# Setup per block of eight row tiles, sums copied bank by bank, last messages written into SBUF: two graph layers on one core

## The chip, the cores and the metric

One Trainium2 chip, one of its cores. The metric is the device time of the whole program in microseconds (us). Its engines are TensorE (PE, with PEld for its weight loads), VectorE (DVE), ScalarE (ACT), GpSimd (POOL) and SyncE (SP), which here only issues loads.

## What is computed

Two layers over 8192 nodes with 128 features, and one 8192 x 8192 adjacency matrix of zeros and ones in float32 (256 MB):

```
h  = relu(layernorm(x));  Wh = h @ W
e  = leaky_relu(Wh@a1 + (Wh@a2).T, 0.2)
att = softmax(where(adj > 0, e, -9e15))
x  = x + relu(att @ Wh)
h  = relu(layernorm(x));  node = h @ W1            # 16 heads
y  = sum over k of node[:, k] * (h @ W2[k])        # the "messages"
x  = x + relu(adj @ y + node @ b)
```

## The kernel before, in words

Rows are cut into 8 blocks (NB) of 8 tiles (T) of 128 rows; NT = 64 tiles. The order on each engine is written out by hand, with semaphores; no scheduler moves anything. A wait on an engine holds all that stands behind it there. There are four stages.

**Setup.** SyncE loads x into `wh` (eight loads), then W, a1, a2, b, W1 and W2, then adj. VectorE takes the statistics of all 64 tiles (L806), aggregates them all (L811), ScalarE takes one square root (L445), then the loop `project` runs over the blocks: VectorE normalises eight tiles into `xn8` (L820), TensorE transposes them (L648), ScalarE applies relu (L451) into `hT4`, TensorE multiplies each tile by `w_sb`, 128 columns (L655), and by `wa` = W [a1 a2], 2 columns (L656), ScalarE copies Wh back over x (L455). Then ScalarE casts the first adj parts to bytes (`cast`, L467, seven times), VectorE finds the extremes of f1 and f2 (L831 to L851), ScalarE takes three exponentials (L485 to L488): `bcol` for the Wh rows, `qcol` and `zcol` for the weights. VectorE multiplies all eight blocks of Wh by `bcol` (L857). `zcol` is transposed, stored to HBM (L495) and read back by GpSimd, spread over all partitions (`load_z`, L401).

**Attention**, 8 target blocks x 4 turns (`IT`) x 2 parts p x 4 chunks k (C). Per chunk TensorE transposes one piece of the byte mask (`turn_mask`, L683), ScalarE evicts it (`evict`, L479), VectorE makes the weights of two source tiles, `p_sb` = max(z, q) times mask (`weigh`, L896), and TensorE adds 2 x 8 products of 129 columns (Wh and the row sum) into three banks `ot_ps` (L734). ScalarE casts adj ahead; it also stores the turned mask to HBM (`maskT_d`, L548) for the second layer. From the second block on the tiles of the block before are finished beside it (`finish_tile`, k = 0 to 3): VectorE divides, adds x (`xt`) and normalises; TensorE multiplies by W1 and W2 (L694, L699); ScalarE scales 16 heads (L525); GpSimd folds them (L381, L384), cuts the message into a high and a low part (L388, L390) and stores it (`msg_d`, L393) with the rows to keep (`keep_d`, L398). `confirm` counts the stores that have landed in `kept`. At a block's end ScalarE copies the three banks to `ut` (L571, in `end_block`), and TensorE clears the banks for the next block (L716, in `start_block`, after the wait on `ot_copied`). ScalarE then loads `xt` for the tiles to finish (L531).

**First gather** (`gather(0, True)`): TensorE multiplies the messages of 64 tiles by masks turned back to float32 (`convert`, L584 and L945) for two of the eight blocks (L774), while the last block's eight tiles are finished, one per seven tiles. `msgs` lies over `wh` and the masks, so SyncE loads messages (L306) once all reads of these are past, eight tiles at a time, each behind its `kept` count. **Three more gathers** of two blocks follow, and the results are turned and added.

## Time and profile before

| | us |
|---|---|
| median of 3 runs (lowest, highest) | 1968.48 (1953.25, 1979.71) |
| profiled execution | 1956.41 |
| its span | 1954.8 |

The mean granted clock of TensorE over the span was 0.983 of full speed. The page gives the busy time of each engine as a share of the span; `PE` records in the timeline carry an `x` count of instruction records, and a float32 matmul leaves two records. A line ends with the idle time before it and what ended that. For stages the order of time is: setup to 121 us, attention from 121.6 to 1405, first gather from 1416 to about 1590, the other gathers to the end.

### The profile page before, as it was taken

The numbers are of one execution on the slowest core, as the hardware profiler recorded it, in microseconds if no ns is written. First come the engines' busy times: TensorE is split into PE (matmuls) and PEld (weight loads), VectorE is DVE, ScalarE is ACT, GpSimd is POOL, SyncE is SP. The second block draws the span as 40 slices with busy tenths as digits, with TensorE's granted clock in tenths as the row PEclk, the third lists the DMA queues.
The fourth block names the chain that finished last, engine by engine and source line by source line (L and its number), as shares of the span: only waits on it lengthen the run. The fifth ranks groups of instructions, "written<-read, shape, count | busy, mean of one in ns | idle before, by whom it ended". The sixth has DMA issues, their size and how long they took to land.

```text
span 1954.8 us, 38986 instructions
## 1 busy us (share of the span) xinstructions
PE 1831.2 (94%) x13412; PEld 1602.2 (82%) x13412; DVE 1206.2 (62%) x1511; ACT 1325.7 (68%) x2127; POOL 698.8 (36%) x533
## 2 busy tenths in 40 slices
PE   1869999999999999999999999999799889999998
PEld 1859988988889888898898898898677568888886
DVE  5356667767767776676676677676656434443434
ACT  1466678778777887787888787778455445555554
POOL 0000025645554554565465465464535400000000
PEclk9979999999999999999999999999999989999999
DMA  8078876776777767767767677673841084444340
GB/s 281 1 275 324 321 307 253 293 283 246 295 268 266 292 248 279 292 248 283 286 259 291 260 278 286 237 288 147 323 166 60 19 330 185 155 168 172 142 180 22
DMA packets 106481, 454.82 MB, mean 233 GB/s; under 512 B 6896, under 2 KB 15296, under 8 KB 88512
## 3 DMA queue, kind: packets, MB, share of 16 engines
q1 hardware_dynamic: 87472, 357.66, 49.4%
q10 hardware_dynamic: 11600, 75.54, 9.3%
q0 software_dynamic: 7360, 20.98, 2.8%
q8 instruction: 30, 0.49, 0.1%
q14 instruction: 19, 0.16, 0.0%
HBM read 366.04 MB, written 88.11 MB: 232 GB/s over the span
## 4 chain that ended last, share of the span: by engine, by line
PE 90%; issue 2%; DMA 2%; ACT 2%; DVE 1%; SPq 1%; POOL 1%; ACTq 0%; DVEq 0%; POOLq 0%
PE ot_ps L734 46%; PE mt_ps L774 12%; PE ot_ps L774 12%; PE hw_ps L699 11%; PE mt_ps L683 6%; PE ot_ps L655 1%; PE h_ps L694 1%; DMA xt<-in_x_dram 1%; ACT prod L525 1%; SPq L278 1%; ACT wh_mask L467 1%; PE mt_ps L648 1%; POOL prod L381 0%; DMA adj_sb<-maskT_d 0%; PE hw_ps L656 0%
## 5 line engine op out<-in xcount | busy, mean ns | idle before, releaser
L734 PE MATMUL ot_ps<-wh_mask,p_sb 128*128 (+1 forms) x8192 | 983.1, 278 | 3.6 <-DVE p_sb L896 3.6
L734 PEld LDWEIGHTS ot_ps<-wh_mask,p_sb 128*128 128x128 f32 x8192 | 945.0, 193 | 5.3 <-issue 3.5
L896 DVE SCALAR_TENSOR_TENSOR p_sb<-zb,qcol,mt 128x1024 f32<-128x1024 uint8 (+1 forms) x512 | 776.0, 1546 | 271.2 <-ACT mt L479 214.2
L381 POOL TENSOR_TENSOR prod<-prod 128x1024 f32<-128x1024 f32 (+2 forms) x192 | 409.2, 2131 | 537.7 <-ACT prod L525 527.3
L467 ACT ACTIVATE wh_mask<-adj_sb 128x2048 uint8<-128x2048 f32 x256 | 491.6, 1926 | 0.0
L584 ACT ACTIVATE mask<-adj_sb 128x1024 fp32r<-128x1024 uint8 x240 | 255.2, 1064 | 196.3 <-PE ot_ps L774 177.6
L479 ACT ACTIVATE mt<-mt_ps 128x1024 uint16<-128x1024 uint16 x256 | 266.8, 1043 | 169.7 <-PE mt_ps L683 160.4
L945 DVE CAST mask<-adj_sb 128x1024 fp32r<-128x1024 uint8 x272 | 200.9, 746 | 270.9 <-PE mt_ps L774 246.4
L525 ACT ACTIVATE prod<-hw_ps,node 128x128 f32<-128x128 f32 x1024 | 277.9, 382 | 100.5 <-PE hw_ps L699 100.5
L774 PE MATMUL mt_ps<-mask,msgs 128*128 128x512 f32 x1024 | 284.3, 400 | 30.0 <-DVE mask L945 29.0
L774 PE MATMUL ot_ps<-mask,msgs 128*128 128x512 f32 x1024 | 276.2, 392 | 0.7
L774 PEld LDWEIGHTS mt_ps<-mask,msgs 128*128 128x128 f32 x1024 | 191.9, 189 | 80.3 <-issue 41.9
L699 PE MATMUL hw_ps<-wcat,hT 128*128 128x512 f32 x512 | 240.7, 593 | 0.0
L774 PEld LDWEIGHTS ot_ps<-mask,msgs 128*128 128x128 f32 x1024 | 192.9, 189 | 43.8 <-issue 3.4
L683 PEld LDWEIGHTS mt_ps<-ident,wh_mask 128*128 128x128 bf16 x2048 | 144.7, 114 | 59.8 <-issue 58.2
L683 PE MATMUL mt_ps<-ident,wh_mask 128*128 128x128 bf16 x2048 | 157.3, 221 | 0.0
L699 PEld LDWEIGHTS hw_ps<-wcat,hT 128*128 128x128 f32 x512 | 88.8, 191 | 61.7 <-issue 61.1
L401 POOL DMA_DIRECT2D zb<-zrow_d x8 | 4.3, 541 | 243.1 <-DVE p_sb L896 131.2
L384 POOL TENSOR_TENSOR msg<-prod 128x128 f32<-128x128 f32 x64 | 80.4, 1256 | 5.0
L390 POOL TENSOR_TENSOR msg<-msg 128x128 fp32r<-128x128 f32 x64 | 71.5, 1117 | 5.1
L388 POOL CAST msg<-msg 128x128 fp32r<-128x128 f32 x64 | 58.3, 911 | 10.7 <-POOL msg L384 10.7
L393 POOL DMA_DIRECT2D msg_d<-msg x64 | 37.8, 590 | 47.2 <-ACT keep L517 25.9
(106 smaller groups left out, 631.5 us busy)
## 6 DMA issues: line engine op xcount, KB each, us to landing
adj_sb<-in_adj_dram SPq DMA_DIRECT2D x128, 2048.0 KB, 8.4
maskT_d<-mt ACTq DMA_DIRECT2D x64, 1024.0 KB, 5.3
adj_sb<-maskT_d SPq DMA_DIRECT2D x32, 2048.0 KB, 8.0
msg_d<-msg POOLq DMA_DIRECT2D x64, 128.0 KB, 6.0
keep_d<-keep POOLq DMA_DIRECT2D x64, 128.0 KB, 6.1
msgs<-msg_d SPq DMA_DIRECT2D x8, 1024.0 KB, 10.0
p_sb<-keep_d SPq DMA_DIRECT2D x4, 2048.0 KB, 12.5
wh_mask<-in_x_dram SPq DMA_DIRECT2D x8, 512.0 KB, 7.2
```

What stands on the lines that cost most here:

```text
L381: pool.tensor_tensor(prod[:, 0:n, :], prod[:, 0:n, :], prod[:, n:2 * n, :], ALU.add)\
L384: pool.tensor_tensor(msg32[:, :], prod[:, 0, :], prod[:, 1, :], ALU.add).then_inc(prod_read, 1)
L467: ins = act.activation(m8[:, q // 2, t:t + HT // 2, :].rearrange("p t n -> p (t n)"), adj_sb[:, q, part * (HT // 2) * BLK:(part + 1) * (HT ...
L479: act.activation(mt[:, p, k, :], mt_ps[k % 2][:, :].bitcast(U16), ACT.Copy).then_inc(evicted, 1)
L525: ins = act.activation(prod[:, head, :], hw_ps[g % 2][:, j * D:(j + 1) * D], ACT.Copy, scale=node[:, head:head + 1])
L584: act.activation(mask32[:, r, ib, :], masks[:, s % 4, ib, t % T // 2, :, t % 2], ACT.Copy)\
L683: ins = pe.transpose(words[:, t * P:(t + 1) * P], m8[:, p, t, :].bitcast(BF16)[:, k:BLK // 2:C], ident16[:, :])
L699: pe.matmul(hw_ps[g % 2][:, :], hT[:, :], wcat[:, g * HB:(g + 1) * HB], start=True, stop=True)\
L734: ins = pe.matmul(ot_ps[h][:, (t - t0) * ROW:(t - t0 + 1) * ROW], p_sb[:, r, t * P:(t + 1) * P], rows, start=False, stop=end and t == t1 - 1)
L774: ins = pe.matmul(acc_ps[2 * ib + h][:, :], msgs[:, t, c, :], mask32[:, r, ib, h * HB:(h + 1) * HB], start=t == 0 and c == 0, stop=t == NT ...
L896: dve.scalar_tensor_tensor(p_sb[:, r, :], zbf[:, bass.ds((ib % 2) * BLK, BLK)], qcol[:, bass.ds(tile + b_, 1)], mtb[:, p, k, :, b_], ALU.m ...
L945: dve.tensor_copy(mask32[:, r, ib, :], masks[:, s % 4, ib, t % T // 2, :, t % 2])\
```

## The change

1. **Setup per block.** Statistics, aggregation and square root are taken block by block, in the order statistics(i+1), norm(i); each x load has its own semaphore. `xn8` has two buffers. `wx_sb` holds W and W [a1 a2] side by side: one matmul of 130 columns per tile instead of two. A row of `whx` is 130 words instead of 129 and holds Wh, f1, f2; `fcol` is a view of it. TensorE turns the next block between the matmuls of this one. ScalarE casts a part of adj after each block from the second on. The parameter loads are issued by ScalarE.
2. **Scaling and z.** VectorE scales Wh blocks 0 and 1, GpSimd blocks 2 to 7; TensorE waits for these from the second turn on. The first block's z rows are spread by eight matmuls into `hw_ps` and two copies, without the trip to HBM.
3. **Block ends.** ScalarE copies each bank when it is done (`copy_sums`, in the last chunk, ahead of the last products), TensorE clears each bank when it is copied. `xt` is loaded one chunk earlier.
4. **Last messages.** For the last eight tiles GpSimd writes the parts straight into `msgs`; TensorE waits for each tile's cut. SyncE loads seven message slots, then the masks, with nothing between.
5. Two mask conversions ahead of the wait for the last sums, on VectorE and ScalarE.

```diff
-        wh_mask = sb("wh_mask", [P, NT * (D + 1) + BLK * T // 2])
+        wh_mask = sb("wh_mask", [P, NT * (D + 2) + BLK * T // 2])
+        wx_sb = sb("wx_sb", [P, D + 2])
...
-        whx = wh_mask[:, 0:NT * (D + 1)].rearrange("p (n f) -> p n f", f=D + 1)
+        whx = wh_mask[:, 0:NT * (D + 2)].rearrange("p (n f) -> p n f", f=D + 2)
+        fcol = whx[:, :, D:D + 2]
...
-            for s in range(NB):
+            for s in range(NB - 1):
                 sp.wait_ge(kept, (s + 1) * T + 2)
                 load_messages(s)
-                if s >= 4:
-                    load_masks(0, s)
+            for s in range(4, NB):
+                load_masks(0, s)
...
+            pool.wait_ge(wh_copied, 3 * NB)
+            pool.wait_ge(setup_act, 7)
+            for i in range(2, NB):
+                rows = wh[:, T * i:T * (i + 1), :]
+                pool.tensor_tensor(rows, rows, bcol[:, T * i:T * (i + 1)].unsqueeze(2).to_broadcast([P, T, D]),
+                                   ALU.mult).then_inc(wh_scaled2, 1)
             pool.wait_ge(z_stored, 16)
-            load_z(0)
...
-            finish_block(NB - 1)
-            confirm(1, IT * NB + 1)
+            for mi in range(T):
+                u, p, m = (NB - 1) * IT + mi // 2, mi % 2, (NB - 1) * T + mi
...
+                fold(m)
+                pool.wait_ge(prod_read, m + 2)
+                pool.tensor_copy(msgs[:, m, 0, :], msg32[:, :]).then_inc(cut_step, 1)
+                pool.wait_ge(cut_step, 2 * m + 1)
+                pool.tensor_tensor(msgs[:, m, 1, :], msg32[:, :], msgs[:, m, 0, :].bitcast(FP32), ALU.subtract)\
+                    .then_inc(cut_step, 1)
...
+            ahead = [(q, part) for q in range(4) for part in range(2 if q < 3 else 1)]
+            deviation(0)
+            for i in range(NB):
+                if i + 1 < NB:
+                    deviation(i + 1)
+                project(i)
+                if i:
+                    cast(*ahead[i - 1], 1, 0)
+            evict(0, 0, 0, 0)
+            evict(1, 1, 0, 0)
...
+            for h in range(2):
+                act.wait_ge(z0_done, h + 1)
+                act.activation(zbf[:, h * HB:(h + 1) * HB], hw_ps[h][:, :], ACT.Copy).then_inc(z0_copied, 1)
...
+            def copy_sums(ib):
+                if not (isinstance(ib, int) and ib == 0):
+                    act.wait_ge(u_read, T * ib)
+                    act.wait_ge(den_read, ib)
+                for h, (t0, t1) in enumerate(GROUPS):
+                    if h < 2:
+                        act.wait_ge(ot_done, 2 * ib + h + 1)
+                    else:
+                        act.wait_ge(p_used[3], 4 * IT * (ib + 1))
+                    act.activation(ut[:, t0:t1, :].rearrange("p t f -> p (t f)"),
+                                   ot_ps[h][:, 0:(t1 - t0) * ROW], ACT.Copy).then_inc(ot_copied, 1)
...
+            def turn_x(i, g):
+                pe.wait_ge(xn8_done, i + 1)
+                if i:
+                    pe.wait_ge(hT_done, 2 * (i - 1) + g + 1)
+                for j in range(4):
+                    ins = pe.transpose(mt_ps[g][:, j * D:(j + 1) * D], xn8[:, i % 2, 4 * g + j, :], ident[:, :])
+                ins.then_inc(xnT_done, 1)
+
             def project(i):
+                for g, (t0, t1) in enumerate(GROUPS):
+                    if i:
+                        pe.wait_ge(wh_copied, 3 * (i - 1) + g + 1)
+                    for t in range(t0, t1):
+                        pe.wait_ge(hT_done, 2 * i + t // 4 + 1)
+                        ins = pe.matmul(ot_ps[g][:, (t - t0) * (D + 2):(t - t0 + 1) * (D + 2)],
+                                        hT4[:, t // 4, t % 4 * P:(t % 4 + 1) * P], wx_sb[:, :], start=True, stop=True)
+                        if t == t1 - 1:
+                            ins.then_inc(wh_done, 1)
+                        if t % 4 == 3 and i + 1 < NB:
+                            turn_x(i + 1, t // 4)
...
             def start_block(ib, last):
-                if not (isinstance(ib, int) and ib == 0):
-                    pe.wait_ge(ot_copied, 3 * ib)
                 for h in range(3):
+                    if not (isinstance(ib, int) and ib == 0):
+                        pe.wait_ge(ot_copied, 3 * ib - 2 + h)
...
+                if not finish and not (isinstance(jg, int) and jg == 0):
+                    pe.wait_ge(wh_scaled2, NB - 2)
...
-                    if t % T == 0:
+                    if s == NB - 1:
+                        pe.wait_ge(cut_step, 2 * t + 2)
+                    elif t % T == 0:
                         pe.wait_ge(msgs_in[s], 16)
```

How the written order moves, at three places. ScalarE in the setup before: after the projection loop come the seven casts (`wh_mask<-adj_sb`), then the exponentials (L485 to L488).

```order
L459 REGISTER_ALU
L459 COMPARE_AND_BRANCH
L467 ACTIVATE wh_mask<-adj_sb 128x2048 x7
L485 ACT_TABLE_LOAD
L485 ACTIVATE bcol<-fcol,shifts 128x64
L486 ACTIVATE qcol<-fcol,shifts 128x64
L488 ACTIVATE zcol<-zcol 128x64
```

ScalarE in the setup now, the last two blocks of the projection and what follows.

```order
L485 ACTIVATE p_sb<-p_sb,eps 128x8
L493 ACTIVATE p_sb,hsum<-mt_ps 128x512 x2
L497 ACTIVATE wh_mask<-ot_ps 128x390 x2
L497 ACTIVATE wh_mask<-ot_ps 128x260
L505 ACTIVATE wh_mask<-adj_sb 128x2048
L493 ACTIVATE p_sb,hsum<-mt_ps 128x512 x2
L497 ACTIVATE wh_mask<-ot_ps 128x390 x2
L497 ACTIVATE wh_mask<-ot_ps 128x260
L505 ACTIVATE wh_mask<-adj_sb 128x2048
L517 ACTIVATE mt<-mt_ps 128x1024 x2
L530 ACT_TABLE_LOAD
L530 ACTIVATE zcol<-zcol 128x64
```

One cast stands behind each block, and the two evictions (L517) are ahead of the exponentials. At the end of a middle block ScalarE had, before, the last products (`prod`), then the copies of the sums (`ut`).

```order
L479 ACTIVATE mt<-mt_ps 128x1024
L522 REGISTER_ALU
L525 ACTIVATE prod<-hw_ps,node 128x128 x4
L522 REGISTER_ALU
L525 ACTIVATE prod<-hw_ps,node 128x128 x4
L566 ISA
L568 REGISTER_ALU
L571 ACTIVATE ut<-ot_ps 128x387 x2
L571 ACTIVATE ut<-ot_ps 128x258
```

Now:

```order
L517 ACTIVATE mt<-mt_ps 128x1024
L585 ISA
L588 ACTIVATE ut<-ot_ps 128x387
L585 REGISTER_ALU
L588 ACTIVATE ut<-ot_ps 128x387
L587 ISA
L588 ACTIVATE ut<-ot_ps 128x258
L568 REGISTER_ALU
L571 ACTIVATE prod<-hw_ps,node 128x128 x4
L568 REGISTER_ALU
L571 ACTIVATE prod<-hw_ps,node 128x128 x4
```

The three copies stand ahead of the last eight products. SyncE at the first gather had, before, masks (`adj_sb<-maskT_d`) between the messages:

```order
L306 DMA msgs<-msg_d 128x2048 x5
L321 DMA adj_sb<-maskT_d 128x2x4096
L306 DMA msgs<-msg_d 128x2048
L321 DMA adj_sb<-maskT_d 128x2x4096
L306 DMA msgs<-msg_d 128x2048
L321 DMA adj_sb<-maskT_d 128x2x4096
L306 DMA msgs<-msg_d 128x2048
L321 DMA adj_sb<-maskT_d 128x2x4096
L327 DMA p_sb<-keep_d 128x4096
```

Now:

```order
L306 DMA msgs<-msg_d 128x2048 x7
L322 DMA adj_sb<-maskT_d 128x2x4096 x4
L328 DMA p_sb<-keep_d 128x4096
```

The last message load is gone, and the four mask loads stand behind the seventh.

## Rows read from the trace of the kernel before

**Rows 1.** The page, busy us of each engine (share of the span) xinstructions.

```profile
PE 1831.2 (94%) x13412; PEld 1602.2 (82%) x13412; DVE 1206.2 (62%) x1511; ACT 1325.7 (68%) x2127; POOL 698.8 (36%) x533
```

**Rows 2.** Timeline of the setup: start us, us, engine, line, out<-in, count.

```profile
18.69 2.03 DVE L806 BATCH_NORM_STATS2 p_sb<-wh_mask  x8 [18.69 <-DMA wh_mask<-in_x_dram]
...
36.37 4.32 DVE L811 BATCH_NORM_AGGREGATE p_sb<-p_sb 128x2 f32<-128x6 f32 x64
...
41.69 2.14 DVE L820 TENSOR_SCALAR p_sb<-wh_mask,p_sb 128x128 f32<-128x128 f32 x8
```

**Rows 3.** Timeline of the projection, at the low and then the full clock.

```profile
53.87 0.60 ACT L451 ACTIVATE p_sb<-mt_ps 128x512 f32<-128x512 f32 x1 [0.45 <-PE mt_ps L648]
...
54.61 0.80 PE L655 MATMUL ot_ps<-w_sb,p_sb 128*128 128x128 f32 x2
...
55.48 0.77 PE L655 MATMUL ot_ps<-w_sb,p_sb 128*128 128x128 f32 x2
...
64.25 0.47 PE L655 MATMUL ot_ps<-w_sb,p_sb 128*128 128x128 f32 x2
...
64.69 0.47 PE L655 MATMUL ot_ps<-w_sb,p_sb 128*128 128x128 f32 x2
```

**Rows 4.** Timeline of the setup's end; the last row is of the chain.

```profile
93.66 12.69 ACT L467 ACTIVATE wh_mask<-adj_sb 128x2048 uint8<-128x2048 f32 x7
...
106.36 1.28 ACT L485 ACT_TABLE_LOAD   x1
...
108.40 9.17 DVE L857 TENSOR_TENSOR wh_mask<-wh_mask,bcol  x8 [11.84 <-ACT zcol L488]
...
121.64 5.75 PE L734 MATMUL ot_ps<-wh_mask,p_sb 128*128 128x129 f32 x32 [1.50 <-DVE p_sb L896]
...
127.84 3.63 PE ot_ps L734 x32
```

**Rows 5.** Timeline of VectorE and GpSimd near 379; last, the page's group of all products.

```profile
377.82 1.25 DVE L896 SCALAR_TENSOR_TENSOR p_sb<-zb,qcol,mt 128x1024 f32<-128x1024 uint8 x1
379.51 2.87 DVE L896 SCALAR_TENSOR_TENSOR p_sb<-zb,qcol,mt 128x1024 f32<-128x1024 uint8 x1 [0.44 <-PE ot_ps L734]
...
378.63 2.66 POOL L381 TENSOR_TENSOR prod<-prod 128x1024 f32<-128x1024 f32 x1 [7.67 <-ACT prod L525]
...
L896 DVE SCALAR_TENSOR_TENSOR p_sb<-zb,qcol,mt 128x1024 f32<-128x1024 uint8 (+1 forms) x512 | 776.0, 1546 | 271.2 <-ACT mt L479 214.2
```

**Rows 6.** Waits of TensorE, 120 to 1400 us: total us, times, longest.

```profile
PE ot_ps L716 <- ACT ut L571: 15.9, 7, 2.4
PE ot_ps L734 <- DVE p_sb L896: 3.6, 6, 1.5
```

**Rows 7.** Timeline at the end of the second block.

```profile
418.49 1.20 ACT L571 ACTIVATE ut<-ot_ps 128x387 f32<-128x387 f32 x3
...
419.75 0.82 PE L716 MATMUL ot_ps<-zeros 128*128 128x512 bf16 x3 [2.45 <-ACT ut L571]
```

**Rows 8.** The chain of waits at the start of the first gather.

```profile
1406.22 8.12 DMA xt<-in_x_dram
...
1416.20 2.04 PE mt_ps L774 x4
...
1421.64 0.93 PE mt_ps L774 x4
```

**Rows 9.** Timeline of TensorE at the last messages.

```profile
1573.15 2.05 PE L774 MATMUL mt_ps<-mask,msgs 128*128 128x512 f32 x4 [18.03 <-DVE mask L945]
```

**Rows 10.** Loads of x and of the messages, by line: ns, first and last start; landing.

```profile
L278 SPq DMA_DIRECT2D wh_mask<-in_x_dram x8: 658/1700/1992, 1.0 to 11.2; - x8
...
DMA to landing us min/median/max: 4.3/7.2/7.8
...
L306 SPq DMA_DIRECT2D msgs<-msg_d x8: 328/448/650, 1404.4 to 1562.4; - x8
...
DMA to landing us min/median/max: 4.9/10.0/14.7
```

More of the change, by code:

```diff
@@ L107, in build @@
         rstd = sb("rstd", [P, 1])
-        fcol = sb("fcol", [P, NT, 2])
         bcol = sb("bcol", [P, NT])
@@ L674, in turn_mask @@
+            for g in range(2):
+                turn_x(0, g)
+            for i in range(NB):
+                project(i)
             def turn_mask(chunk, k, p, casts):
@@ L685, in turn_mask @@
                 ins.then_inc(turned, 1)
+            pe.wait_ge(hT_done, 2 * NB)
             turn_mask(0, 0, 0, 1)
             turn_mask(1, 1, 0, 1)
+            pe.wait_ge(setup_dve, 4)
+            pe.transpose(h_ps[0:2, 0:P], ext[:, :], ident[:, :]).then_inc(setup_pe, 1)
+            pe.wait_ge(setup_dve, 6)
+            pe.matmul(h_ps[:, HB // 2:HB // 2 + 2], ones[0:2, :], extd[:, :], start=True, stop=True)\
+              .then_inc(setup_pe, 1)
+            pe.wait_ge(setup_act, 5)
+            for t in range(T):
+                ins = pe.matmul(hw_ps[t // 4][:, t % 4 * P:(t % 4 + 1) * P], zcol[:, t:t + 1].to_broadcast([P, P]),
+                                ident[:, :], start=True, stop=True)
+                if t % 4 == 3:
+                    ins.then_inc(z0_done, 1)
+            pe.wait_ge(setup_dve, 13)
+            pe.matmul(h_ps[:, 0:D], hrep[:, :], w_sb[:, :], start=True, stop=True).then_inc(setup_pe, 1)
+            pe.transpose(h_ps[0:NT, D:D + P], zcol[:, :], ident[:, :]).then_inc(setup_pe, 1)
             def finish_tile(k, m, pb):
@@ L735, in turn @@
                                                     p_sb[:, r, t * P:(t + 1) * P], rows, start=False, stop=end and t == t1 - 1)
+                                if end and h < 2:
+                                    ins.then_inc(ot_done, 1)
                             ins.then_inc(p_used[r], 1)
@@ L824, in norm @@
                 ins.then_inc(xn8_done, 1)
-            norm(0)
-            with dve.Fori(1, NB) as i:
+            statistics(0)
+            for i in range(NB):
+                if i + 1 < NB:
+                    statistics(i + 1)
                 norm(i)
-            dve.wait_ge(wh_done, 2 * NB)
-            dve.tensor_copy(fcol[:, :, :].rearrange("p n c -> p (n c)"), hw_ps[0][:, 0:2 * NT]).then_inc(setup_dve, 1)
-            dve.wait_ge(setup_dve, 1)
+            dve.wait_ge(wh_copied, 3 * NB)
@@ L922, in start_weights, with convert @@
                     weigh(NB * ib, IT * ib, ib, 0, 0, b_, 0)
+            def convert(ii, first, t):
+                s, r = t // T, t % 2
+                for ib in range(2):
+                    if on_dve(first, t, ib):
+                        dve.wait_ge(masks_in[s % 4], 16 * (ii * (NB // 4) + s // 4 + 1))
+                        if not (first and t < 2):
+                            dve.wait_ge(conv_used[r][ib], ii * (NT // 2) + t // 2)
+                        dve.tensor_copy(mask32[:, r, ib, :], masks[:, s % 4, ib, t % T // 2, :, t % 2])\
+                           .then_inc(conv_dve, 1)
             def end_block(ib):
@@ L936, in _ @@
             attention_loop(dve, turn, None, end_block, alone=True)
-            def convert(ii, first, t):
-                s, r = t // T, t % 2
-                for ib in range(2):
-                    if on_dve(first, t, ib):
-                        dve.wait_ge(masks_in[s % 4], 16 * (ii * (NB // 4) + s // 4 + 1))
-                        if not (first and t < 2):
-                            dve.wait_ge(conv_used[r][ib], ii * (NT // 2) + t // 2)
-                        dve.tensor_copy(mask32[:, r, ib, :], masks[:, s % 4, ib, t % T // 2, :, t % 2])\
-                           .then_inc(conv_dve, 1)
             def take_bank(ii, ib):
```

217 lines of the change are left out of this document (106 added, 111 removed).

## Prediction, made before the changed kernel ran

> **What bounds the kernel now.** I read the page first: TensorE is busy for 94% of the 1954.8 us span [rows 1]. Whatever lies beside a busy TensorE is free; a gain must come out of the other 6% (some 124 us), so the next view is the timeline, to find where those idle stretches are. There are four kinds, and the change touches each.
>
> The setup is the largest. VectorE begins statistics at 18.69, once all of x has landed, aggregates in one go at 36.37 and normalises the first block at 41.69 [rows 2]; TensorE begins its eight blocks only after that, and each block takes it 8.8 us at first, 5.1 later. Then seven casts of adj stand alone on ScalarE from 93.66, the exponentials behind them, eight scalings of the Wh rows on VectorE behind those, and the first attention matmul is at 121.64, at the low clock: its 32 records take 5.75 us where later ones take 3.63 [rows 4]. I measure the setup to the start of the second chunk, 127.84.
>
> Inside the attention, the waits of TensorE between 120 and 1400 sum up to 15.9 us in 7 times for the copy of the sums and 3.6 us in 6 times for weights [rows 6]. At a block's end ScalarE scales eight products and then copies three banks in 1.20 us, and only then does TensorE zero the banks [rows 7]. Before the first gather the chain runs over the load of xt, 8.12 us, and the gather starts at 1416.20 at the low clock (2.04 us against 0.93 for four records) [rows 8]. In the middle of the first gather TensorE stands for 18.03 us, until the last messages and masks have come back from HBM [rows 9].
>
> **Setup.** The first sqrt needs the parameters, now issued on ScalarE's queue from 1.0 us instead of at 12.9. The x loads landed in 4.3 to 7.8 us [rows 10]; the last of five issues at about 4.6, so the parameters are in at 9 to 12.4. Behind them come the small matmuls (2.9 us between 19.5 and 22.4 in the timeline), a table load 1.28, sqrt and reciprocal about 0.9, eight normalisations 2.14 and a first group of transposes 1.0: the first relu is at 17.5 to 20.5; I take 18.
>
> A block's chain on ScalarE and TensorE at the low clock: relu 0.60 and 0.15 to the matmul [rows 3]; row tiles start 0.86 apart there because each has a 128 column and a 2 column matmul, so I take half, 0.43, for one of 130 columns, 3.4 for eight; a group of four transposes between, 1.0; latency and last copy 0.5: 5.6. Then a cast, 12.69/7 = 1.8, and the next sqrt with its wait, 0.4: **7.9 us**. At the full clock row tiles start 0.44 apart [rows 3], so 0.22 each: 0.75 + 1.8 + 0.5 + 0.5 + 1.8 + 0.4 = **5.7 us**. VectorE needs 2.03 + 4.32/8 + 2.14 + 0.5 = 5.2 us per block [rows 2], just below both, so it is not the limit, but is close behind it. Before, the low clock held for 20 us after TensorE's first block (from 43.9 in the timeline to 64 [rows 3]); I take the same here, three blocks. Block 0 has no cast: 6. So 18 + 6 + 2x7.9 + 4x5.7 + 3.5 = 66 for the last copy (59 if all at the full clock, 77 if none).
>
> Behind it: the seventh cast 1.8, two evictions 1.94, table load 1.28, three exponentials about 0.9: bcol is ready at B = 72 (65 to 83). The zrow trip to HBM, its load and six of eight scalings leave this chain; the z rows come by eight matmuls and two copies, which run beside VectorE's two scalings (before: 9.17/8 = 1.15 each). Uncontended, the first weights would be ready at B + 2.3 + 0.2 + 1.28 = B + 3.8, and with a first chunk at the low clock (6.2 us, as from 121.64 to 127.84) the second chunk starts at B + 10.
>
> But now GpSimd scales six blocks at the same time. The row: a GpSimd add of 1024 elements held from 378.63 to 381.29, VectorE's product of the same size began at 379.51 and took 2.87 instead of 1.25; it ended 1.1 us after GpSimd [rows 5]. So they take turns, 2.66 + 1.25 = 3.9 us a pair. Six GpSimd scalings then lie between VectorE's two scalings, copy and first four products: the fourth is ready at B + 6x2.66 + 6x1.25 + 0.2 = B + 23.6, and the second chunk, which needs it half way, counts as started at B + 21.6. Price between 0 and 11.6 us. I take the whole, because that row shows full turns: 72 + 21.6 = 93.6, so the setup **gains 34** (23 with low clock throughout; 53 with the full clock and no collision). On TensorE the wait for GpSimd's six (wh_scaled2) is hidden behind the first turn, 8 chunks of 4.07 us; without that cover it would cost up to 23 us.
>
> The Trainium skill, "SBUF — State Buffer", section "SBUF: two separate sides", says that the port pair which VectorE and GpSimd share is an exclusive lock: the one that starts second is blocked for the whole of the other's instruction. By that rule the price is the full 11.6 us. The mean over the attention [rows 5] (1546 ns per product, of which GpSimd was busy beside only some) would make it 0.3 us for each of the six products and scalings, under 2 us; the pair of rows agrees with the rule, so I follow it.
>
> **Block boundaries.** The copies of banks 0 and 1 now run under the last eight matmuls, that of bank 2 (0.4 us) under the four hw_ps matmuls that follow, before ScalarE scales the last products; the xt load is issued two chunks earlier. ScalarE now waits at the third bank with eight product scalings, GpSimd's fold and the next eviction queued behind: the hw_ps results come only 0.9 us later, so it costs them nothing. Of 15.9 + 3.6 I take **17** (14 to 19.5); the first boundary has no hw_ps matmuls and keeps some 0.4.
>
> **Start of the gather.** xt is loaded ahead and the first masks are converted before the sums are awaited. Late next: the first message load, issued at 1404.4 after the last p_used; the quickest of these landed in 4.9 us [rows 10], so the gather starts at 1409.3 instead of 1416.2: **7** (4 if that load takes longer, 10 if the four remaining idle microseconds keep the clock up, worth 1.7).
>
> **End of the messages.** The last eight tiles' messages are written by GpSimd into the buffer that TensorE reads, and the masks of the last slot are no longer behind them on SP. GpSimd's last fold and cut ended at about 1559.0, TensorE would want that tile as its last of eight, at 1555.1 + 7x1.83 = 1568, so 9 us of cover. The 18.03 and the low clock behind it (2.05 + 1.5 against 1.84, 1.7) go: **19.5** (17 to 20).
>
> Nothing is charged for fewer matmuls in the setup outside the chain above, nor for strided fcol reads (64 elements, 0.2 us).
>
> Sum: 34 + 17 + 7 + 19.5 = 77.5. The profiled execution took 1956.4, so 1879. It lies 12 below the median of the three runs, 1968.5, and these spread by 26, so I give 1880.
>
> **Rivals.**
> 1. *The clock stays low through the whole projection.* For it: TensorE will be busy only 5.4 of 7.9 us a block, less than in the phase where it took 20 us to rise. The setup gains 23: 1890. Chance 0.17.
> 2. *GpSimd hardly collides.* Its scalings are bounded by the start of the first turn at low clock, where a weight is wanted only every 4 us, as slow as the turns. The setup gains 46: 1867. Chance 0.18.
> 3. *The casts inside the blocks wait for adj.* adj landed from 28 on; now issued some 4 us earlier, the first cast wants it at about 30. If the loads come 5 to 10 us late, ScalarE stands with relu and copies queued behind: gain 20, 1893. Chance 0.07.
> 4. *GpSimd cuts the last messages too late.* The cover of 9 us is used up if every fold meets VectorE: 5 given back, 1884. Chance 0.05.
> 5. *The copies do not run ahead.* If ScalarE reaches them late (its queue has an eviction and a cast ahead), the boundaries keep their 17: 1896. Chance 0.03.
> 6. *Slower: the stride.* The rows that the 8192 attention records read are now 520 bytes apart, not 516. Each record starts 3.63/32 = 113 ns after the last. If the new stride cost 9.5 ns a record, all of the gain would be gone; beyond that the kernel is slower, at 20 ns by 86 us, 2043. Against it: the 516 byte rows already start at every multiple of 4 bytes, the 520 byte ones at a part of these. Chance 0.02.
>
> The forecast has the remaining 0.48.
>
> **How the numbers follow.** Cases 1 to 5 lie between 1867 and 1896; unknown prices (53 at one end of the setup, 20 at the other) and the 12 us between profile and median widen this to **1855 to 1908**, which leaves out the stride, some of cases 3 and 5 together, and a setup better than any bound. A change of 2% is about what a measurement of this kernel can tell from none: 39 us, at 1929. Only the stride or several of the small cases with most of the setup lost lie above it: faster 0.95, within 2% 0.04, slower 0.01.
>
> **What would show it.** First attention matmul at about 85, the second chunk's steady pace at 94; VectorE products of 2.9 us there, beside GpSimd scalings; a block of the projection every 8, then 6 us; the wait of TensorE for the sums near 1 us in all; no DMA of xt on the chain; the gather at 4 us after the last hw_ps matmul; no wait over 2 us in the first gather. Wrong it would be most of all in B: a start at 75 or at 105 moves the time by the same amount.

## The result, and the profile after

The changed kernel took **1878.7 us** (median of 4 runs, 1875.0 to 1880.3) beside 1973.2 for the kernel before on the same chip (1953.3 to 1979.7): a ratio of **0.9535, with a 95% interval of 0.9462 to 0.9608**. Faster, as forecast. The profiled execution has a span of 1873.4 us, 81.4 less than before; TensorE's busy share rose from 94% [rows 1] to 97%. The page after, engines and the group of the attention matmuls:

```profile
PE 1814.5 (97%) x13300; PEld 1586.9 (85%) x13300; DVE 1210.6 (65%) x1511; ACT 1330.3 (71%) x2144; POOL 715.7 (38%) x530
...
L796 PE MATMUL ot_ps<-wh_mask,p_sb 128*128 (+1 forms) x8192 | 980.2, 277 | 6.4 <-DVE p_sb L961 6.4
```

I cut both spans at the same events of TensorE. The third attention chunk is the first that runs at the steady pace in both (94.33 after), so "start of the second chunk" is that less one period of 4.07:

| stretch of the span | before | after | gain | forecast |
|---|---|---|---|---|
| start to second attention chunk | 127.84 | 90.26 | 37.6 | 34 |
| to the last hw_ps group of the attention | 1276.3 | 1260.3 | 16.0 | 17 |
| to the first matmul of the gather | 12.1 | 5.2 | 6.9 | 7 |
| to the first turned result of the gather | 177.4 | 156.4 | 21.0 | 19.5 |
| to the end | 361.2 | 361.3 | -0.1 | 0 |

**The setup after**, timeline. First all that answers to [rows 2, 3]: statistics start with the first load, and each block has a relu, two groups of row tiles and a cast.

```profile
6.46 1.65 DVE L872 BATCH_NORM_STATS2 p_sb<-wh_mask 128x6 f32<-128x128 f32 x8 [6.46 <-DMA wh_mask<-in_x_dram]
...
18.01 0.60 ACT L493 ACTIVATE p_sb<-mt_ps 128x512 f32<-128x512 f32 x1 [3.49 <-PE mt_ps L699]
...
31.09 0.59 ACT L493 ACTIVATE p_sb<-mt_ps 128x512 f32<-128x512 f32 x1
...
31.91 2.07 PE L708 MATMUL ot_ps<-wx_sb,p_sb 128*128 128x130 f32 x8 [2.70 <-ACT p_sb L493]
...
34.63 1.23 PE L708 MATMUL ot_ps<-wx_sb,p_sb 128*128 128x130 f32 x8
...
36.18 1.90 ACT L505 ACTIVATE wh_mask<-adj_sb 128x2048 uint8<-128x2048 f32 x1
...
38.17 0.59 ACT L493 ACTIVATE p_sb<-mt_ps 128x512 f32<-128x512 f32 x1
...
45.94 1.13 PE L708 MATMUL ot_ps<-wx_sb,p_sb 128*128 128x130 f32 x8 [2.70 <-ACT p_sb L493]
```

The first relu is at 18.01, as forecast, and a block takes 7.1 us here (6.8 on average). The first eight records take 2.07, the next eight 1.23: TensorE has stood for 2.70 beside ScalarE's cast, and comes back at half speed. It does so behind four of the six such gaps; behind the other two, the one before 45.94 for instance, the first eight records take 1.13. Then the setup's end, which answers to [rows 4]:

```profile
74.09 0.40 ACT L533 ACTIVATE bcol<-wh_mask,shifts 128x64 f32<-128x64 f32 x1
74.52 4.06 DVE L922 TENSOR_TENSOR wh_mask<-wh_mask,bcol 128x1024 f32<-128x1024 f32 x2 [2.55 <-ACT bcol L533]
74.66 16.04 POOL L414 TENSOR_TENSOR wh_mask<-wh_mask,bcol 128x1024 f32<-128x1024 f32 x6 [64.82 <-ACT bcol L533]
...
80.30 16.26 DVE L961 SCALAR_TENSOR_TENSOR p_sb<-zb,qcol,mt 128x1024 f32<-128x1024 f32 x8
...
83.32 5.19 PE L796 MATMUL ot_ps<-wh_mask,p_sb 128*128 128x129 f32 x32 [0.47 <-DVE p_sb L961]
...
91.84 2.05 PE L796 MATMUL ot_ps<-wh_mask,p_sb 128*128 128x129 f32 x16 [0.79 <-DVE p_sb L961]
```

Six scalings on GpSimd take 16.04. Five of the records last 2.87, each with a wait for a VectorE operation in it, and where a product of VectorE lies between two of them they start 2.84 apart (at 82.15 and 84.99, for instance). The third, at 80.29, finds VectorE's copy just done and takes 1.90.

**A block boundary after** (the end of the second block, which answers to [rows 7]), timeline:

```profile
375.96 1.21 ACT L588 ACTIVATE ut<-ot_ps 128x387 f32<-128x387 f32 x3
375.97 1.88 PE L760 MATMUL hw_ps<-wcat,hT 128*128 128x512 f32 x4
377.69 0.81 PE L776 MATMUL ot_ps<-zeros 128*128 128x512 bf16 x3
...
379.39 4.96 POOL L378 TENSOR_TENSOR prod<-prod 128x1024 f32<-128x1024 f32 x3 [6.94 <-ACT prod L571]
379.88 2.40 DVE L937 TENSOR_SCALAR att<-att,rden 128x128 f32<-128x128 f32 x1
...
385.67 2.05 PE L796 MATMUL ot_ps<-wh_mask,p_sb 128*128 x16 [0.81 <-DVE p_sb L961]
```

The copies run under the hw_ps matmuls, and the zeroing starts with no wait. What is late next stands below it: VectorE's small division of 128 elements in each partition begins just behind GpSimd's fold, takes 2.40, and the weights that follow it reach TensorE 0.81 late. Waits of TensorE after, from 120 to 1345 us, in all (before, [rows 6]: 15.9 + 3.6):

```profile
PE ot_ps L796 <- DVE p_sb L961: 5.1, 8, 0.8
```

**The gather after**, timeline, which answers to [rows 8, 9]: the message loads are issued 0.3 us after the last hw_ps group starts; the last tile's message is in SBUF at 1498.5, and TensorE runs through the last slot.

```profile
1350.55 1.88 PE L760 MATMUL hw_ps<-wcat,hT 128*128 128x512 f32 x4
1350.87 2.93 SPq L306 DMA_DIRECT2D msgs<-msg_d  x6
...
1355.73 1.87 PE L840 MATMUL mt_ps<-mask,msgs 128*128 128x512 f32 x4 [3.30 <-issue]
...
1498.07 0.46 POOL L454 TENSOR_TENSOR msgs<-msg,msgs 128x128 fp32r<-128x128 f32 x1
...
1508.39 1.17 PE L840 MATMUL mt_ps<-mask,msgs 128*128 128x512 f32 x4 [0.29 <-DVE prod L1023]
```

### The profile page after: what moved, and what is told of

Read it like the earlier page. It is cut to its first block, busy times and chain, and to the rows that moved or that the text cites. A ratio compares the mean times of both kernels' runs of the same rounds, so it can differ in the third digit from the quotient of the medians.

```text
span 1873.4 us, 38193 instructions
## 1 busy us (share of the span) xinstructions
PE 1814.5 (97%) x13300; PEld 1586.9 (85%) x13300; DVE 1210.6 (65%) x1511; ACT 1330.3 (71%) x2144; POOL 715.7 (38%) x530
## 4 chain that ended last, share of the span: by engine, by line
PE 90%; DVE 4%; ACT 3%; issue 2%; DMA 1%; POOL 1%; ACTq 0%; DVEq 0%; POOLq 0%
PE ot_ps L796 45%; PE mt_ps L840 13%; PE ot_ps L840 13%; PE hw_ps L760 11%; PE mt_ps L728 5%; ACT wh_mask L505 1%; DVE p_sb L961 1%; PE h_ps L755 1%; PE ot_ps L708 1%; DVE att L937 1%; ACT prod L571 1%; DVE p_sb L887 0%; DVE keep L942 0%; DMA keep_d<-keep 0%; PE h_ps L767 0%
## 5 line engine op out<-in xcount | busy, mean ns | idle before, releaser
L517 ACT ACTIVATE mt<-mt_ps 128x1024 uint16<-128x1024 uint16 x256 | 267.6, 1046 | 151.8 <-PE mt_ps L728 150.5
L728 PE MATMUL mt_ps<-ident,wh_mask 128*128 128x128 bf16 x2048 | 156.4, 219 | 0.0
L954 DVE TENSOR_SCALAR xn<-keep,mv,rstd 128x128 f32<-128x128 f32 x64 | 51.7, 809 | 2.3
```

The costliest lines, as they stand in the source:

```text
L517: act.activation(mt[:, p, k, :], mt_ps[k % 2][:, :].bitcast(U16), ACT.Copy).then_inc(evicted, 1)
L728: ins = pe.transpose(words[:, t * P:(t + 1) * P], m8[:, p, t, :].bitcast(BF16)[:, k:BLK // 2:C], ident16[:, :])
```

## The experiments

A time without a range is that of one execution; the kernel before took 1978.4 (median of 7) beside the first four and 1964.5 (of 7) beside the others, which ran on another chip. What tells them apart are the landmarks: B, the end of the exponential that gives bcol (74.49 after), the third attention chunk (94.33), the last hw_ps group (1350.55) and the gather's first matmul (1355.73).

**e1: no scaling on GpSimd.**

```diff
-            for i in range(2, NB):
-                rows = wh[:, T * i:T * (i + 1), :]
...
-            for i in range(2):
+            def scale(i, done):
...
+            for i in range(NB):
+                scale(i, wh_scaled if i < 2 else wh_scaled2)
```

> All eight scalings of the Wh rows go back to VectorE, ahead of the copy of bcol; GpSimd scales none. The rest is the changed kernel. There bcol is ready at 74.5 us (B), the first attention matmul stands at 83.3 (B + 8.8) and the second chunk counts as started at 90.3 (B + 15.8). Turn-taking theory: without GpSimd each scaling takes 1.2, so the first product is ready at B + 8 x 1.2 + 0.2 + 1.3 = B + 11.2, and with a first chunk at the low clock (6.2) the second chunk starts at B + 17.4, only 1.6 later than in the changed kernel: moving six scalings to GpSimd was worth 1.6 us, not the 7.3 us of VectorE time that they cost. Rival (GpSimd's part is nearly free, and what delays the start is something else): the second chunk starts 6 to 7 us later than in the changed kernel.

1878.7 us. Timeline of VectorE:

```profile
77.29 9.17 DVE L916 TENSOR_TENSOR wh_mask<-wh_mask,bcol 128x1024 f32<-128x1024 f32 x8 [2.27 <-ACT bcol L527]
```

B was 77.26 and the third chunk at 97.56, B + 20.3, where the changed kernel has B + 19.8. Giving six scalings to GpSimd is worth half a microsecond, less than the 1.6 that I had expected and far from the rival's 6 to 7: eight on VectorE take 9.17 in one piece, and taking turns costs about as much. The first chunk starts at B + 11.6 instead of B + 8.8, but its 32 records then take 4.21 instead of 5.19, and no weights are late in the second.

**e2: GpSimd begins its scalings later**, behind four attention products.

```diff
             pool.wait_ge(setup_act, 7)
+            pool.wait_ge(p_ready, 4)
             for i in range(2, NB):
```

> GpSimd's six scalings wait until the first four products are made. Turn-taking theory: VectorE's two scalings, copy and first product are alone, first product ready at the second z copy + 1.3 = B + 5.2 (changed kernel B + 8.8), VectorE scalings 1.2 each instead of 2.0, but the six GpSimd operations (2.66 each) now fall beside later products, which take 2.9 to 3.9 each: TensorE, which wants one product per 2.04, is held there for up to 6 x 1.8 = 11 us less the products made ahead. Second chunk near B + 11.5, but the eighth chunk no earlier than in the changed kernel (within 2 us). Rival (no contention): first and eighth chunk both 3.6 earlier.

1871.3 us. GpSimd in the timeline, and TensorE at the sixth chunk:

```profile
84.52 16.97 POOL L415 TENSOR_TENSOR wh_mask<-wh_mask,bcol 128x1024 f32<-128x1024 f32 x6 [74.82 <-DVE p_sb L962]
...
102.63 3.84 PE L797 MATMUL ot_ps<-wh_mask,p_sb 128*128 128x129 f32 x32 [0.34 <-DVE p_sb L962]
```

The first chunk starts at 80.81, B + 4.7, so the uncontended start of B + 3.8 was nearly right. The collision moves to the next chunks, with a pair every 2.84 us; but the sixth chunk starts at B + 26.5 and in the changed kernel at B + 31.9, the eighth at B + 34.7 and B + 40.0. I had expected no gain at the eighth, and 5.3 us came: a pair of 2.84 for a weight that is wanted every 2.04 costs only 0.8, half a chunk of lead absorbs some of it, and 1.5 is speed: the first chunk's records take 3.84 instead of 5.19.

**e3: scalings one by one inside the first turn**, on VectorE, each behind the two products of a chunk (4 executions).

```diff
+                        if not finish and isinstance(jg, int) and jg == 0 and C * p + k + 1 < NB:
+                            scale(C * p + k + 1, wh_scaled2)
```

> GpSimd scales nothing. VectorE scales block 0, copies bcol, makes the first products, and scales one more block behind each of the seven next chunks, in its own idle time (it needs 2 x 1.28 of 4.07 us a chunk, a scaling 1.2). Turn-taking theory: first attention matmul at the second z copy + 1.3 = B + 5.2, second chunk at B + 11.4 against B + 15.8, no product over 1.3 us in the first turn, TensorE never waits there: 4.4 us faster than the changed kernel, all of it at the start. Rival (the low clock bounds the start): the first chunk takes longer at the low clock and less than 2 us remain. Rival (VectorE has no room): products late in the first turn, the gain is lost by the ninth chunk.

**1872.3 us** (1871.5 to 1874.5), ratio 0.9509 (0.9424 to 0.9594): against before clearly faster, against the changed kernel not told apart by the ratios, so I go by the trace. VectorE and TensorE in the timeline:

```profile
83.59 1.22 DVE L918 TENSOR_TENSOR wh_mask<-wh_mask,bcol 128x1024 f32<-128x1024 f32 x1
84.72 2.47 DVE L958 SCALAR_TENSOR_TENSOR p_sb<-zb,qcol,mt 128x1024 f32<-128x1024 f32 x2
...
87.04 3.79 PE L792 MATMUL ot_ps<-wh_mask,p_sb 128*128 128x129 f32 x32
```

The third chunk is at 91.28, B + 14.1: 5.7 us better than the changed kernel, 6.2 better than e1. Two products and a scaling are 3.7 of a chunk's 4.07 us, so nothing waits. I had expected 4.4. The first chunk starts 3.1 us sooner after B; 1.6 of the rest is that it runs at full speed (its records take 3.79 instead of 5.19), which I had not counted, and 1.1 that the second chunk's weights are not late.

**e4: all casts behind the projection.**

```diff
                 project(i)
-                if i:
-                    cast(*ahead[i - 1], 1, 0)
+            for part in ahead:
+                cast(*part, 1, 0)
```

> The seven casts of adj stand behind the projection again, not one behind each block. In the changed kernel a block takes 6.8 us on average, and the chain runs through its cast of 1.8 us. Theory (a cast inside a block is on the chain, not hidden): the block period falls to VectorE's 4.9 to 5.3 us, last copy 7 x 1.6 = 11 us earlier, then 12.7 us of casts ahead of the exponentials: bcol within 3 us of 74.5. Rival (the casts are hidden in the blocks): the period stays over 6.3 and bcol comes 10 to 12 us later.

1870.3 us. Two neighbouring blocks of ScalarE's timeline, and the casts:

```profile
22.58 0.59 ACT L493 ACTIVATE p_sb<-mt_ps 128x512 f32<-128x512 f32 x1
...
27.21 0.59 ACT L493 ACTIVATE p_sb<-mt_ps 128x512 f32<-128x512 f32 x1
...
53.35 12.69 ACT L505 ACTIVATE wh_mask<-adj_sb 128x2048 uint8<-128x2048 f32 x7
```

Without casts a block takes 4.63 us, at full speed from 21.01 on, and the copies end at 53.35 instead of 68.7: 15.3 won, and 10.8 paid behind (12.69, of which the changed kernel has its seventh cast there anyway). B is 70.05. So the six casts that the change puts into the projection lose 4.4 us: each costs its 1.9 on the chain and opens a gap behind which, four times of six, TensorE is slow. I had expected the periods to stay at VectorE's 4.9 to 5.3 and bcol to move by less than 3 us.

**e5: both products before the division**, at the one place where fold and division meet.

```diff
                             weigh(n, i, ib, p, k, 0, tile)
+                        both = finish and p == 0 and k == 1 and isinstance(jg, int) and jg == 0
+                        if both:
+                            weigh(n, i, ib, p, k, 1, tile)
                         if finish and k < 3:
...
-                        if not weighed:
+                        if not weighed and not both:
                             weigh(n, i, ib, p, k, 1, tile)
```

> In the first turn of each later block VectorE makes both products of the second chunk before it divides and normalises the first tile; before, division and normalisation stood between the two. In the changed kernel TensorE still waits there 0.8 us in each of six blocks, because VectorE's division of 128 elements (0.3 alone) takes 2.4 beside GpSimd's fold. Theory: those waits go, 5 us (attention from the third chunk to the last hw_ps matmul 4 to 5 us shorter). Rival: the transpose of the normalised tile, which TensorE wants in the third chunk, is now 1.3 us late and TensorE waits there instead: nothing gained.

1874.9 us. TensorE's waits for weights from 200 to 1400 us fall from 5.1 in 8 times to

```profile
PE ot_ps L796 <- DVE p_sb L961: 2.3, 7, 0.5
```

and the stretch from the third chunk to the last hw_ps group is 1253.0 instead of 1256.2, 3.2 shorter: less than the 4 to 5 expected, since 2.3 us of waits remain.

**e6: e3 and e5 together, four casts behind the projection and three behind the z rows** (4 executions). The edits of e3 and e5 are not shown again.

```diff
+            for part in ahead[:4]:
+                cast(*part, 1, 0)
             evict(0, 0, 0, 0)
...
             act.dma_start(zrow_d, zT[:, :]).then_inc(z_stored, 16)
+            for part in ahead[4:]:
+                cast(*part, 1, 0)
```

> Three edits together on the changed kernel: VectorE spreads the scalings (as in e3), both products first (as in e5), and of the casts of adj none inside the projection, four behind it and the last three behind the z rows. Theory: blocks of the projection every 4.6 us as in e4, last copy at 53, four casts 7.3, two evictions 1.8, table load and exponentials 2.1: bcol ready at 65 (changed kernel 74.5, e4 70.0). First attention matmul at B + 5.9, third chunk at B + 14.1 = 79 against 94.3: 15 faster at the start, 5 more from the block starts, 1858 in all. Rival: the three late casts hold the eviction for the third chunk, and TensorE or VectorE waits there 3 to 5 us. Rival: the low clock returns while TensorE idles behind the projection, first chunk 2 to 4 us longer.

**1859.6 us** (1858.2 to 1861.8), **ratio 0.9464 (0.9414 to 0.9513)**: the fastest kernel of this study. Its median is some 19 us below the changed one's, which was taken at another time, and the two ratios' intervals overlap; between the profiled executions the difference is 14.8. ScalarE and TensorE in the timeline:

```profile
72.79 3.81 PE L794 MATMUL ot_ps<-wh_mask,p_sb 128*128 128x129 f32 x32
73.85 5.51 ACT L499 ACTIVATE wh_mask<-adj_sb 128x2048 uint8<-128x2048 f32 x3 [0.69 <-ACT small L535]
...
79.27 1.00 ACT L511 ACTIVATE mt<-mt_ps 128x1024 uint16<-128x1024 uint16 x1
...
82.17 0.61 PE L724 MATMUL mt_ps<-ident,wh_mask 128*128 128x128 bf16 x8 [1.50 <-issue]
```

B is 67.46, 2.5 later than expected; the third chunk is at 82.78, 11.6 earlier than in the changed kernel, and the rest of the attention 3.5 shorter. The three late casts hold up an eviction (79.27), for which TensorE waits 1.5: the rival of the expectation, at a small price. This wait I did not remove.

**e7: the three copies of the sums at the end of the block again.**

```diff
-                        if ends_block(jg) and p == 1 and k == 3:
-                            copy_sums(ib)
...
+            def end_block(ib):
+                act.wait_ge(p_used[3], 4 * IT * (ib + 1))
+                copy_sums(ib)
...
+                if not (isinstance(ib, int) and ib == 0):
+                    pe.wait_ge(ot_copied, 3 * ib)
                 for h in range(3):
```

> One part of the change undone: ScalarE copies the three banks after everything else of the block, as before, and TensorE waits for all three before it clears the first. xt is still loaded early. Theory (the boundary gain is the copies): TensorE waits 2.4 us at six boundaries and 1.2 at the first, as before, attention from the second chunk to the last hw_ps matmul 12 to 16 us longer than in the changed kernel (1260.3); start of the gather 1 to 2 us later. Rival (TensorE's wait before was for xt and VectorE): under 5 us longer.

1893.7 us. TensorE's waits from 120 to 1400 us, then its timeline at the end of the second block, and the granted clock there (stretch, length, busy, clock, DMA share, GB/s):

```profile
PE ot_ps L778 <- ACT ut L588: 15.9, 7, 2.4
PE ot_ps L798 <- DVE p_sb L963: 2.0, 6, 0.5
```

```profile
383.18 0.82 PE L778 MATMUL ot_ps<-zeros 128*128 128x512 bf16 x3 [2.45 <-ACT ut L588]
...
384.56 5.16 PE L798 MATMUL ot_ps<-wh_mask,p_sb 128*128 x32
```

```profile
383.00:386.00 3.00, 2.82 (x18) 0.66 0.00 0
```

The wait of [rows 6] is back to the tenth, and the stretch from the third chunk to the last hw_ps group is 16.5 longer (1272.7), just above the 12 to 16 that I expected; the gather's start is 0.2 later, not 1 to 2. It is 15.9 for the waits, less 3.1 since the new weight waits go, and 3.4 for two chunks: the one at 384.56, which takes 5.16 instead of 3.79 at a granted clock of 0.66, and one at 879.61, each with slower transposes ahead of it. Behind the other five stops the chunk takes 3.79. The kernel before has the same picture: behind five of its seven stops the chunk takes 3.79, behind the two at 749 and 1244 it takes 5.43.

```profile
750.09 5.43 PE L734 MATMUL ot_ps<-wh_mask,p_sb 128*128 x32
```

**e8: xt loaded after the block's end again.**

```diff
-                        if ends_block(jg) and p == 1 and k == 2:
-                            load_xt(ib)
...
+            def start_block(ib, last):
+                if not (isinstance(ib, int) and ib == 0):
+                    load_xt(ib - 1)
```

> One part undone: xt is loaded by ScalarE after the block, as before; copies bank by bank as in the change. Theory: at the first boundaries up to 1 us each for VectorE's wait for xt (load lands in 3.4), so attention 0 to 4 us longer. At the gather TensorE does not need xt to start, only masks and messages, and the masks of the first two tiles are now made ahead: its start moves by under 1 us, but the first tile's normalised rows come some 6 us late, and TensorE waits for them in the second gather step: 3 to 5 us lost there. Rival (the masks made ahead are not what frees the start): the gather starts 6 us later, as before.

1882.4 us. The last load of xt is issued 1.9 us behind the last hw_ps group, in the changed kernel 12.6 ahead of it (some three chunks earlier, not the one that the list of changes says). The gather starts 5.3 us after that group, against 5.2: so xt had left that chain by the order of the gather's start, and not by its earlier load. The price is elsewhere, 2.8 in the attention and 2.2 in the gather, where I had expected 3 to 5. Timeline of TensorE at both places:

```profile
228.76 2.05 PE L799 MATMUL ot_ps<-wh_mask,p_sb 128*128 x16 [2.98 <-DVE p_sb L964]
...
1367.72 0.33 PE L770 MATMUL h_ps<-ident,xn 128*128 128x128 f32 x1 [1.36 <-DVE xn L957]
```

At the end of the first block VectorE stands 4.98 us for xt, with the weights of the next chunk queued behind it; in the gather it stands 8.22, and the first tile's normalised row comes late.

**e9: the last block's messages through HBM again**, with the masks of slots 4 to 7 still ahead of them.

```diff
             for s in range(4, NB):
                 load_masks(0, s)
+            sp.wait_ge(kept, NB * T + 2)
+            load_messages(NB - 1)
...
-                pool.tensor_copy(msgs[:, m, 0, :], msg32[:, :]).then_inc(cut_step, 1)
...
+            finish_block(NB - 1)
+            confirm(1, IT * NB + 1)
...
-                    if s == NB - 1:
-                        pe.wait_ge(cut_step, 2 * t + 2)
```

> Only the end of the messages is undone: the last block's eight messages go to HBM and come back in one load, as before the change; the masks of slots 4 to 7 are still loaded ahead of them. My theory (the gain of 21.2 us in the first gather is mostly the store and the load of the last messages): in the trace of the changed kernel the last message is cut at 1498.5, and TensorE wants it near 1506; with a store and a load behind the cut (landing 4.9 us for a load of messages, 2 to 4 for a store and the semaphores between) plus the deferred masks' work the wait comes back as one stop of 8 to 14 us on TensorE at the first matmul of the last slot, and the first gather (first gather matmul to first turned result) takes 165 to 171 instead of 156.4; total 1882 to 1888 in span. Rival A (the old wait of 18.0 was the masks, queued on SP behind the messages, and not the messages): no stop over 2 us, first gather 156 to 158, span 1873. Rival B (nothing of the old wait was the masks): the whole 18 comes back, first gather 174 to 178, span 1891 to 1895.

1896.3 us. TensorE in the timeline, and the clock behind the stop:

```profile
1446.91 1.17 PE L817 MATMUL mt_ps<-mask,msgs 128*128 128x512 f32 x4 [2.71 <-DVE mask L976]
...
1512.30 2.04 PE L817 MATMUL mt_ps<-mask,msgs 128*128 128x512 f32 x4 [12.57 <-DMA msgs<-msg_d]
```

```profile
1512.00:1516.00 4.00, 3.70 (x9) 0.50 1.01 434
```

The stop is in my range, but the first gather takes 174.0, 17.6 more than in the changed kernel, above the 165 to 171 that I gave and inside the 174 to 178 of rival B. The stop itself speaks against rival B, which wants the whole 18 back. The 17.6 is three things: 12.57 of stop, 2.4 behind it (the first four groups take 6.0 instead of 3.6, at the halved clock), and a wait of 2.71 for a mask conversion at 1446.91, 65 us ahead of the stop, where VectorE's two conversions beside GpSimd's fold take 4.55. The trace of the changed kernel has no such wait and that of the kernel before one of 0.73; why it is 2.71 here stays open. So some 15 of the 21.0 are shown for the direct write, and the order of the masks is worth some 5 (18.03 of stop [rows 9] against 12.57).

**e10: two operands, 128 and 2 columns, again.**

```diff
-                        ins = pe.matmul(ot_ps[g][:, (t - t0) * (D + 2):(t - t0 + 1) * (D + 2)],
-                                        hT4[:, t // 4, t % 4 * P:(t % 4 + 1) * P], wx_sb[:, :], start=True, stop=True)
...
+                        pe.matmul(ot_ps[g][:, at:at + D], rows, w_sb, start=True, stop=True)
+                        ins = pe.matmul(ot_ps[g][:, at + D:at + D + 2], rows, wa, start=True, stop=True)
```

> Only the 130 column operand is undone: each row tile's projection is a matmul of 128 columns and one of 2, with two weight loads, as before; all else of the changed setup stays. My theory (a row tile costs two times a two-pass matmul of about 128 columns: 0.43 us at the full clock and 0.86 at the low, where the changed kernel shows 0.13 to 0.26 a tile): TensorE's work in a block of eight rises by 1 to 2.5 us, and as the chain of a block holds TensorE's matmuls with ScalarE's copies behind them, the block's period goes from 6.8 to 8 to 9 us; last copy of the projection at 78 to 86 instead of 68.7, third attention chunk at 104 to 112 instead of 94.3, span 1883 to 1891. Rival (the block is bound by ScalarE's copies and casts, and TensorE's extra weight loads and matmuls run beside them): period 6.8 to 7.2, third chunk at 94 to 97, span 1873 to 1876.

1907.4 us. The third chunk is at 125.33, **31.0 later** than in the changed kernel; the rest is alike (1255.9 to the last hw_ps group). Timeline of TensorE, two neighbouring row tiles, the first attention chunk, and the column of the granted clock:

```profile
28.30 0.77 PE L710 MATMUL ot_ps<-wx_sb,p_sb 128*128 128x128 f32 x2
28.66 0.55 PEld L711 LDWEIGHTS ot_ps<-wx_sb,p_sb 128*128 128x128 f32 x2
28.87 0.42 PE L711 MATMUL ot_ps<-wx_sb,p_sb 128*128 128x2 f32 x2
29.09 0.55 PEld L710 LDWEIGHTS ot_ps<-wx_sb,p_sb 128*128 128x128 f32 x2
29.16 0.78 PE L710 MATMUL ot_ps<-wx_sb,p_sb 128*128 128x128 f32 x2
...
114.32 6.47 PE L798 MATMUL ot_ps<-wh_mask,p_sb 128*128 128x129 f32 x32 [1.51 <-DVE p_sb L963]
```

```profile
60.00:68.00 8.00, 8.00 (x39) 1.00 0.00 1
```

I had expected 10 to 18 us, from the matmul count at the speeds of the changed kernel. But a row tile takes 0.86 us in every block, twice the 0.44 of [rows 3], to the end of the projection, and a block 10.8: TensorE did not come to full speed there. In the changed kernel it did, at 25 us, with its second block. In this one execution the single operand is worth 31.0 of the setup's 37.6, by fewer matmuls and by the clock together; how much is which I did not separate. That the operand decides the clock is likely but not shown: the kernel before has the same two operands and reached full speed in its trace, after 20 us.

## Why the prediction was right, point by point

**Setup, 34 forecast, 37.6 measured.** Start (18), full collision and low first chunk all came; two sizes were off and cancel in part.
- *Turn-taking.* The step "2.66 + 1.25 = 3.9 us a pair" was mis-sized: a pair takes 2.84. I took GpSimd's part from a fold add of [rows 5]. That record held some wait, but little: a fold add of the same size at 1552.94 in the kernel before, with nothing on VectorE beside it, takes 2.39. A scaling without a rival takes 1.90, so it is another operation's price that I used. So the second chunk is at B + 15.8 instead of B + 21.6. The mechanism held: VectorE's products take 2.9 beside GpSimd's scalings and 1.2 without them (e3), as the rule in the Trainium skill, "SBUF — State Buffer", section "SBUF: two separate sides", says: who starts second waits for the other's end. By it, and by the runs, six scalings handed to GpSimd buy nothing (e1), and the way to win 5.7 is to place them in VectorE's own gaps (e3).
- *B, 72 forecast, 74.5 measured*, and 76.1 to 77.8 in e1, e2, e3, e5, e7, e8 and e9, whose projection is the same: the profiled changed kernel was the earliest of them. The term "2x7.9 + 4x5.7" was the wrong picture: the clock neither stayed low for 20 us nor stayed high; it rose within 9 us and then fell in four of the six casts' gaps, which gives blocks of 6.4 to 7.1, 6.8 on average, where my term has a mean of 6.4. The sum came out near by the mean, not by the mechanism.
- *The largest piece I did not set apart.* I priced one operand at half a row tile, 3.4 us a block at the low clock and half that at the full one. In e10, without it, a block takes 4.0 us more and the setup 31, the clock being low throughout.

**Boundaries, 17 forecast, 16.0 measured.** e7 gives 16.5 for the copies alone. I named the wait for the sums, and the trace shows none. Two misses beside it cancel. Of the 3.6 us of weights that I counted among what goes, 1.5 is the wait ahead of the first chunk [rows 4], which belongs to the setup; the other 2.1 did not go, but grew to 5.1 by a collision that my list of what is late next lacked: the fold of GpSimd with the division of VectorE, 0.8 us of TensorE in five blocks and 0.4 in a sixth (e5: 3.2 us); 0.8 more is late in the last block. And I counted nothing for the clock: the slow chunks behind two of the old stops cost 3.3. So 15.9 + 3.3 - 3.0 = 16.2.

**Start of the gather, 7 forecast, 6.9 measured**, by all signs through the message load, as said: it is issued at 1350.87, 4.9 before the first matmul, and the quickest of these loads lands in 4.5. The profile names no releaser there. **End of the messages, 19.5 forecast, 21.0 measured**: the cut came at 1498.5, 8 us before TensorE wanted it near 1506, against my cover of 9. The old stop and the slow groups behind it were 18.0 + 1.6, as I took them; 0.7 more is a wait for a mask conversion that the kernel before has at 1469.6, and 0.7 was not traced.

**The rivals.** Clock low throughout: not so, though e10 shows that it was near, one operand away. GpSimd hardly collides: it does. Casts waiting for adj: no wait. Messages cut too late, copies that do not run ahead: neither. The stride: 32 records start in 3.63 us in the steady chunks after as in [rows 4], so nothing per record.

The forecast sum is 77.5, the measured 81.4 in the profiles. The median of 1878.7 against my 1880 is luck beyond that: my base was a profiled execution of 1956.4, while the kernel before had a median of 1973.2 beside this one. From the medians the gain is 94.5; where the other executions of the kernel before spend their extra time was not traced. Their clock figures give a hint. Of the fourteen executions beside the experiments, the nine of 1956 to 1972 us have a mean granted clock of 0.980 to 0.982, and the five of 1978 to 1982 us, though longer, one of 0.987 to 0.991. A projection at half speed to its end, under a column that reads 1.00 there, would look like that (e10: 0.995), and five blocks at 8.8 instead of 5.1 us are 18.5 us by estimate. If so, part of the 94.5 is the operand of e10, and e10's 31 us may differ from one execution to the next. No trace here shows either.

## What to carry to other kernels

A gap on TensorE costs its own length and often a half-speed stretch behind it. Here a stop of 2.5 us at a boundary cost 1.6 to 1.7 more twice in seven (the kernel before and e7), so some 0.5 on average; a gap of 2.7 in the projection did so four times of six; and one of 12.6 cost 2.4 more (e9). Price a short operation put "for free" into such a gap by what it does to the gap (e4). Handing work from VectorE to GpSimd gained almost nothing here (0.5 us for six scalings, e1), since VectorE was the one awaited and they take turns; look for slack in VectorE's own schedule, one operation per period, first. And take a duration for a sum from a record that has nothing beside it.

## What the runs showed that I had not expected

- A matmul of two columns is as dear as one of 128 in e10: its weight load starts at 28.66 and that of the next tile at 29.09, 0.43 later, half of a tile's 0.86. The records of its weight load (0.55) are as long as those of the wide one.
- The column of the granted clock reads 1.00 in stretches in which TensorE runs at half speed: e10 from 60 to 68 us, with row tiles 0.86 apart, and the kernel before near 54 us [rows 3]. In both this is before the column's first change (after 112 us in e10, after 93 us in the kernel before, which went to full speed at 64 us under a steady 1.00). Behind that change the column and the durations agree. Early in a program I read the speed from the durations of equal matmuls.
- The projection with 130 columns reached full speed 5 to 9 us after its first transposes in all ten traces that have it (at 21.01 in e4, at 25.47 in the changed kernel, whose programs are the same up to there). With 128 and 2 columns the kernel before took 20 us of work with hardly a gap. e10 had 20 us of such work as well, then a gap of 2.2 us in each block, and did not get there in the projection. Two traces against ten; what in the two matmuls delays the rise was not tested.
